# A recommendation tower on one core: two selected pairs of unit 1 go in front, into the banks of the turns, and the last unit's grams get other neighbours

## The chip, the cores and the metric

The kernel runs on one core of one Trainium2 chip. The metric is the device time of one execution in microseconds. Three executions of the kernel before took 426.69, 427.25 and 428.56 us; the median, 427.25 us, is the time before.

## The reference

2048 samples, 32 fields. Every sample takes one row of 64 numbers from each of 32 tables, forms the inner products of all pairs of these 32 rows, and puts them with 16 dense features through a tower of three layers.

```python
e = jnp.stack([tbl_0[ids[:, 0]], ..., tbl_31[ids[:, 31]]], axis=1)   # (2048, 32, 64)
gram = jnp.einsum('bnd,bmd->bnm', e, e)
rows, cols = jnp.triu_indices(32, k=1)
z = gram[:, rows, cols]                                              # 496 products per sample
h = jnp.concatenate([z, dense_ctx], axis=1)                          # 512
h = jnp.maximum(h @ W_top1 + b_top1, 0.0)                            # 512 -> 512
h = jnp.maximum(h @ W_top2 + b_top2, 0.0)                            # 512 -> 256
y = h @ W_top3                                                       # 256 -> 1
```

All numbers are float32. 20 of the tables have 1000 or 1250 rows, 12 are looked up by address.

## The kernel before, in words

The batch is cut into four units of 512 samples (UNITS, UNIT). For each unit the engines do five things.

**Selected fields.** The 20 small tables lie in the on-chip memory, each split into three bf16 parts. VectorE writes one-hot matrices (`one_hots`, a ring of four pieces), and TensorE multiplies them with the tables (`select(u, g)`). Fields go in ten pairs, g = 0 to 9; a pair is worked in two halves. The first seven pairs have 24 matmuls in a half, the last three 30. A pair fills one bank of the accumulator memory. `sel_bank` says which: the two banks of `sel_ps` in turn, but for unit 1's pairs 2 and 3, which go to the two banks of `tower_ps`. ScalarE copies a bank to `vecs` (`selected`, four copies) and counts `sel_emptied`.

**Gathered fields.** GpSimd issues 48 gathers per unit (`gather`, numbered 0 to 191 through the kernel); TensorE transposes the rows in three turns per round (`turn(u, r, x)`, r = 0, 1), into the two banks of `gat_ps`, and ScalarE copies them out (`gathered`, counting `gat_emptied`). After each gather stand some tiny memsets (`spacer`) that hold the next one back. The table `BEHIND` names gathers that wait until a given chunk of grams (unit, round, chunk) is done.

**Grams.** `gram(u, r, c)` is a chunk of 64 small float32 matmuls of 32x32, which the trace shows as 128 matmul records, since each is carried out in two parts. Four chunks make a round, two rounds a unit. Two chunks fill `gram_ps`, which ScalarE, and VectorE for some, copy out.

**The way through HBM.** SyncE's queue writes the products of a unit (`rows_out`, 12 transfers) and reads their diagonals back as `z` (`rows_back`, one transfer of dense features, five of diagonals). The last unit does this round by round, so it has two passes of the tower, of 256 samples each; they are passes 3 and 4, which the code calls LAST and LAST + 1. `rows_back` of either waits until all four blocks of layer 1 of pass 2 are computed, and for the products.

**The tower.** `layer1(v, j)`, j = 0 to 3, `layer2(v, o)`, o = 0, 1, and `layer3(v)`, in the two banks of `tower_ps`, with ScalarE taking each result out.

The order on every engine is written out by hand. TensorE's puts tower work or selects of the next unit between the chunks of grams. In unit 0 every one of the eight chunks has one half of a select of unit 1 ahead of it, so pairs 0 to 3 of unit 1 are done by the end of unit 0's grams (L588 to L600). ScalarE starts to empty them only when the last chunk of unit 0 is done, because the grams still read `vecs` (`act.wait_ge(gram_full, ...)` in its unit loop). `select(1, 4)`, the next work of TensorE, waits for the bank of pair (1, 0) to be emptied (L497, L498). In unit 3, the last, each chunk has half a block of layer 1 of pass 2 ahead of it; layers 2 and 3 of pass 2 follow the last chunk, and then passes 3 and 4.

## Time and profile before

| | us |
|---|---|
| median of three executions | 427.25 |
| the profiled execution | 428.72 |
| its span, first to last instruction | 426.9 |
| TensorE busy | 384.3 (90%) |
| GpSimd busy | 277.2 (65%) |
| VectorE busy | 230.6 (54%) |
| ScalarE busy | 166.6 (39%) |
| mean granted TensorE clock | 0.992 of 2.4 GHz |

All stretches below are in microseconds from the start of the span. An engine's busy time counts instructions that run; the number in square brackets at the end of a row is how long the engine was idle before it, and what ended that. Where the profile finds no releaser it says "issue".

### The profile page before, as it was taken

How to read it: one execution, taken by the hardware profiler on the slowest of the kernel's cores; microseconds unless marked ns; L12 is line 12 of the kernel's file. 1: busy time of each engine (PE TensorE's matmuls, PEld its weight loads, DVE VectorE, ACT ScalarE, POOL GpSimd, SP SyncE). 2: the span in 40 equal slices, each digit the busy share in tenths (PEclk: the TensorE clock that was granted, in tenths of full speed). 3: DMA queues.
4: the chain of work that ended last, by engine and by line, in shares of the span. 5: the costliest groups of instructions: out<-in, count | busy, mean ns of one | idle time of the engine just before them, and what ended most of it. 6: DMA issues, size and time to landing. Idle time of an engine off the chain costs nothing.

```text
span 426.9 us, 15066 instructions
## 1 busy us (share of the span) xinstructions
PE 384.3 (90%) x6516; PEld 216.1 (51%) x6516; DVE 230.6 (54%) x717; ACT 166.6 (39%) x264; POOL 277.2 (65%) x748
## 2 busy tenths in 40 slices
PE   0677868999959999999999999999999999888998
PEld 0343434555535555555545555566445554555576
DVE  2999999863445987006258987007158982001000
ACT  4347576322128425230354425230354425131222
POOL 6888889854548888556578988555588988300000
PEclk9999999999997999999999999999999999999999
DMA  5953941300107781100077721011077111034510
GB/s 178 381 156 100 302 119 38 73 19 15 20 18 140 161 267 44 20 18 17 17 139 154 227 69 47 16 21 18 18 148 170 28 21 23 14 56 97 96 49 0
DMA packets 38236, 37.51 MB, mean 88 GB/s; under 512 B 13781, under 2 KB 26903, under 8 KB 38042
## 3 DMA queue, kind: packets, MB, share of 16 engines
q1 hardware_dynamic: 31594, 29.04, 27.0%
q0 software_dynamic: 6144, 6.30, 7.2%
q10 hardware_dynamic: 432, 1.21, 0.8%
q8 instruction: 51, 0.84, 0.8%
q14 instruction: 15, 0.12, 0.1%
HBM read 28.45 MB, written 8.09 MB: 86 GB/s over the span
## 4 chain that ended last, share of the span: by engine, by line
PE 76%; DVE 14%; issue 4%; ACT 3%; DMA 2%; DVEq 0%
PE sel_ps L511 40%; PE tower_ps L555 13%; DVE onehot L458 10%; PE gram_ps L540 10%; PE tower_ps L565 6%; PE gat_ps L525 3%; PE tower_ps L511 3%; DVE tabs L446 2%; ACT vecs L321 2%; PE tower_ps L574 2%; DVE work L441 2%; DMA ids_wide<-ids_scratch 1%; DMA ids_scratch<-sel_f 1%; DMA sel_ids<-in_ids_sel_dram 1%; ACT tabs L314 0%
## 5 line engine op out<-in xcount | busy, mean ns | idle before, releaser
L458 DVE TENSOR_SCALAR onehot<-ids_wide,row_ids 128x512 bf16<-128x512 f16 x688 | 202.0, 365 | 99.1 <-PE sel_ps L511 80.5
L511 PE MATMUL sel_ps<-onehot,tabs 128*64 128x512 bf16 x1968 | 224.9, 385 | 31.7 <-DVE onehot L458 16.2
L284 POOL DMA_INDIRECT rows<-in_tbl_dram,gat_ids x192 | 195.2, 1017 | 75.7 <-PE gram_ps L540 54.8
L511 PEld LDWEIGHTS sel_ps<-onehot,tabs 128*64 128x64 bf16 x1968 | 117.7, 111 | 133.6 <-issue 36.5
L321 ACT COPY vecs<-sel_ps 64x256 f32<-64x256 f32 x152 | 92.1, 606 | 102.7 <-PE sel_ps L511 58.4
L280 POOL MEMSET spare<- 128x1 f32 x548 | 81.8, 149 | 20.6
L555 PE MATMUL tower_ps<-work,w_sb 128*128 128x512 f32 (+1 forms) x160 | 59.4, 516 | 0.0
L540 PEld LDWEIGHTS gram_ps<-vecs 64*32 64x32 f32 x4096 | 38.9, 105 | 29.8 <-issue 27.0
L540 PE MATMUL gram_ps<-vecs 64*32 64x32 f32 x4096 | 43.9, 201 | 8.1 <-issue 7.1
L555 PEld LDWEIGHTS tower_ps<-work,w_sb 128*128 128x128 f32 x160 | 28.9, 190 | 18.6 <-issue 16.6
L465 DVE COPY work<-gram_ps 128x512 f32<-128x512 f32 x8 | 5.2, 688 | 56.6 <-PE gram_ps L540 56.6
L344 ACT ACTIVATE h<-tower_ps,b_sb 128x512 f32<-128x512 f32 (+1 forms) x20 | 12.0, 602 | 51.6 <-PE tower_ps L555 51.6
L565 PE MATMUL tower_ps<-h,w_sb 128*128 128x512 f32 (+1 forms) x80 | 29.7, 516 | 0.0
L338 ACT COPY work<-gram_ps 128x512 f32<-128x512 f32 x24 | 13.0, 589 | 39.0 <-PE gram_ps L540 39.0
L314 ACT CAST tabs<-work 128x1024 bf16<-128x1024 f32 (+1 forms) x10 | 11.1, 1109 | 25.2 <-DVE work L441 19.5
L329 ACT COPY vecs<-gat_ps 128x512 f32<-128x512 f32 x24 | 13.8, 594 | 14.6 <-PE gat_ps L525 14.3
L565 PEld LDWEIGHTS tower_ps<-h,w_sb 128*128 128x128 f32 x80 | 14.6, 190 | 9.2 <-issue 8.1
L525 PE MATMUL gat_ps<-ident,rows 128*128 128x128 f32 x96 | 14.9, 284 | 0.7 <-ACT vecs L329 0.7
L441 DVE TENSOR_TENSOR work<-work,tabs 128x1024 f32<-128x1024 f32 (+1 forms) x10 | 12.9, 1294 | 2.8 <-ACT tabs L309 2.8
L525 PEld LDWEIGHTS gat_ps<-ident,rows 128*128 128x128 f32 x96 | 10.1, 140 | 7.0 <-issue 5.8
L446 DVE TENSOR_TENSOR tabs<-work,tabs 128x1024 bf16<-128x1024 f32 (+1 forms) x10 | 12.9, 1294 | 1.1 <-ACT tabs L314 1.1
L309 ACT CAST tabs<-work 128x1024 bf16<-128x1024 f32 (+1 forms) x10 | 11.1, 1108 | 5.0 <-DMA work<-in_packed_dram 4.8
(16 smaller groups left out, 41.4 us busy)
## 6 DMA issues: line engine op xcount, KB each, us to landing
ids_wide<-ids_scratch SPq DMA_DIRECT2D x40, 256.0 KB
rows<-in_tbl_dram,gat_ids POOLq DMA_INDIRECT x192
products<-work SPq DMA_DIRECT2D x12, 248.0 KB
products<-work SPq DMA_DIRECT2D x24, 120.0 KB
work<-in_packed_dram SPq DMA_DIRECT2D x5, 512.0 KB
work<-products SPq DMA_DIRECT2D x9, 256.0 KB
work<-in_packed_dram SPq DMA_DIRECT2D x3, 640.0 KB
work<-in_packed_dram ACTq DMA_DIRECT2D x2, 512.0 KB
```

Of the source, the lines that this page charges most:

```text
L280: nc.gpsimd.memset(spare[:], 0.0).then_inc(spaced, 1)
L284: nc.gpsimd.indirect_dma_start(out=rows[:, r, k, h, :], out_offset=None, in_=tables[GATHERED[k]], in_offset=bass.IndirectOffsetOnAxis(ap=g ...
L321: last = nc.scalar.copy(vecs[DIM * h:DIM * h + DIM, :, N_GAT + 2 * g + at], sel_bank(u, g)[DIM * at:DIM * at + DIM, HALF * h:HALF * h + HALF])
L329: nc.scalar.copy(vecs[:, P * r:P * r + P, at:at + fields], gat_ps[:, n % 2, 0:P * fields].rearrange("p (f j) -> p j f", f=fields))\
L441: nc.vector.tensor_tensor(piece, piece, tabs[:, c0:c0 + k, 0, :], ALU.subtract).then_inc(rest_ready, 1)
L446: nc.vector.tensor_tensor(tabs[:, c0:c0 + k, 2, :], stage[g % STAGE_SLOTS][:, 0:k, :], tabs[:, c0:c0 + k, 1, :], ALU.subtract).then_inc(ta ...
L458: last = nc.vector.tensor_scalar(onehot[:, n % RING, c - c0, :], ids_wide[:, k, :], row_ids[chunks[k]][:, c:c + 1], None, ALU.is_equal)
L511: last[at] = nc.tensor.matmul(sel_bank(u, g)[DIM * at:DIM * at + DIM, :], tabs[:, first_chunk[k] + c, part, :], onehot[:, piece_no(u, g, h ...
L525: last = nc.tensor.transpose(gat_ps[:, n % 2, P * at:P * at + P], rows[:, r, k, :, :].rearrange("p h d -> p (h d)"), ident[:])
L540: last = nc.tensor.matmul(gram_ps[32 * s:32 * s + 32, h, i, :], v, v, start=True, stop=True, skip_group_check=True)
L555: last = nc.tensor.matmul(tower_ps[:, (v + j) % 2, 0:width], w1_sb[:, c, P * j:P * j + P], z[:, c, x0:x0 + width], start=(c == 0), stop=(c ...
L565: last = nc.tensor.matmul(tower_ps[:, (v + o) % 2, 0:width], w2_sb[:, j, P * o:P * o + P], h1[:, j, 0:width], start=(j == 0), stop=(j == J ...
```

## The change

Two edits, and the tables that follow from them.

**Unit 1.** `sel_bank` puts pairs 4 and 5 of unit 1 into the banks of `gat_ps`, whose last turn of unit 0 comes before. TensorE's order in round 1 of unit 0 now holds pairs 2 and 3, pair 4 and pair 5 of unit 1: pair 2 whole ahead of chunk 0, then a half ahead of each of chunks 1 to 3, then one and a half pairs behind. The first two turns of unit 1 wait until ScalarE has emptied pairs 4 and 5; pairs 6 and 7 wait for the banks of pairs 0 and 1. VectorE copies the last two chunks of unit 0 out between the halves of pair 5, not of pair 4.

**Last unit.** A whole block of layer 1 of pass 2 stands ahead of each chunk of round 0, and layer 2 and layer 3 of pass 2 are spread ahead of the four chunks of round 1 and of its last. ScalarE's order follows.

**Gathers.** The gates in `BEHIND` move by one or two gathers. Gathers 48 to 63 have one memset behind them (48 to 61 before), 64 to 88 two (three before).

```diff
-NEAR_SPACERS, SPACERS = 1, 3
-NEAR_SPACED = range(48, 62)
+SPACERS = 3
+FEWER = {**dict.fromkeys(range(48, 64), 1), **dict.fromkeys(range(64, 89), 2)}
...
-          56: (0, 1, 0), 58: (0, 1, 1), 60: (0, 1, 2), 62: (0, 1, 3),
+          58: (0, 1, 0), 60: (0, 1, 1), 62: (0, 1, 2), 64: (0, 1, 3),
...
-            return tower_ps[:, g - 2, :] if u == 1 and g in (2, 3) else sel_ps[:, sel_no(u, g) % 2, :]
+            if u == 1 and g in (2, 3):
+                return tower_ps[:, g - 2, :]
+            if u == 1 and g in (4, 5):
+                return gat_ps[:, g - 4, :]
+            return sel_ps[:, sel_no(u, g) % 2, :]
...
+                    layer2(u - 1, (0,))
                 gram(u, 1, 0, (0, 1) if u < LAST else (0,))
                 if u == LAST:
-                    layer1(u - 1, 3)
+                    layer2(u - 1, (1,))
+                    layer3(u - 1)
                     gram(u, 1, 1, (0,))
...
-                    if u == 1 and g == 4:
+                    if u == 1 and g == 5:
                         gram(0, 1, 1, (0, 1))
...
                 if u == 1 and g in (4, 5) and parts[0] == 0:
-                    pe.wait_ge(sel_emptied, n - 3)
+                    pe.wait_ge(gat_emptied, gat_no(0, 1, N_TURNS - 1) + 1)
+                elif u == 1 and g in (6, 7) and parts[0] == 0:
+                    pe.wait_ge(sel_emptied, n - 5)
...
-                if n >= 2:
+                if u == 1 and r == 0 and x < 2:
+                    pe.wait_ge(sel_emptied, sel_no(1, 5 if n % 2 == 1 else 4) + 1)
+                elif n >= 2:
                     pe.wait_ge(gat_emptied, n - 1)
...
                     for c in range(CHUNKS):
-                        layer1(u - 1, c // 2, (c % 2,))
+                        layer1(u - 1, c)
                         gram(u, 0, c)
                     for x in range(N_TURNS):
                         turn(u, 1, x)
-            for c in range(CHUNKS):
-                layer1(LAST - 1, 2 + c // 2, (c % 2,))
-                gram(LAST, 1, c)
+                    layer2(u - 1, 0)
+                    gram(u, 1, 0)
+                    layer2(u - 1, 1, range(0, J1 // 2))
+                    gram(u, 1, 1)
+                    layer2(u - 1, 1, range(J1 // 2, J1))
+                    gram(u, 1, 2)
+                    layer3(u - 1)
+                    gram(u, 1, 3)
```

TensorE, round 1 of unit 0 in the order before: after the last chunk of round 0, one half of a select (24 matmuls) ahead of each of four chunks, and then pairs 4 to 7 in `sel_ps` up to the first turn of unit 1.

```order
L511 MATMUL tower_ps<-onehot,tabs 64x512 x24
L540 MATMUL gram_ps<-vecs 32x32 x64
L511 MATMUL tower_ps<-onehot,tabs 64x512 x24
L540 MATMUL gram_ps<-vecs 32x32 x64
L511 MATMUL tower_ps<-onehot,tabs 64x512 x24
L540 MATMUL gram_ps<-vecs 32x32 x64
L511 MATMUL tower_ps<-onehot,tabs 64x512 x24
L540 MATMUL gram_ps<-vecs 32x32 x64
L511 MATMUL sel_ps<-onehot,tabs 64x512 x204
```

The same place in the order after; `gat_ps` holds pairs 4 and 5.

```order
L513 MATMUL tower_ps<-onehot,tabs 64x512 x48
L544 MATMUL gram_ps<-vecs 32x32 x64
L513 MATMUL tower_ps<-onehot,tabs 64x512 x24
L544 MATMUL gram_ps<-vecs 32x32 x64
L513 MATMUL tower_ps<-onehot,tabs 64x512 x24
L544 MATMUL gram_ps<-vecs 32x32 x64
L513 MATMUL gat_ps<-onehot,tabs 64x512 x24
L544 MATMUL gram_ps<-vecs 32x32 x64
L513 MATMUL gat_ps<-onehot,tabs 64x512 x72
L513 MATMUL sel_ps<-onehot,tabs 64x512 x108
```

One more half stands ahead of the last chunk, and behind it three more halves need no bank that ScalarE has yet to empty.

TensorE, round 1 of the last unit in the order before, from its transposes to layer 1 of pass 3 (L555 is layer 1, L565 layer 2, L574 layer 3).

```order
L525 MATMUL gat_ps<-ident,rows 128x128 x12
L555 MATMUL tower_ps<-work,w_sb 128x512 x2
L540 MATMUL gram_ps<-vecs 32x32 x64
L555 MATMUL tower_ps<-work,w_sb 128x512 x2
L540 MATMUL gram_ps<-vecs 32x32 x64
L555 MATMUL tower_ps<-work,w_sb 128x512 x2
L540 MATMUL gram_ps<-vecs 32x32 x64
L555 MATMUL tower_ps<-work,w_sb 128x512 x2
L540 MATMUL gram_ps<-vecs 32x32 x64
L565 MATMUL tower_ps<-h,w_sb 128x512 x8
L574 MATMUL tower_ps<-h,w_sb 1x512 x2
L555 MATMUL tower_ps<-work,w_sb 128x256 x16
```

The same place after (L559, L569, L578 are the three layers).

```order
L559 MATMUL tower_ps<-work,w_sb 128x512 x4
L544 MATMUL gram_ps<-vecs 32x32 x64
L529 MATMUL gat_ps<-ident,rows 128x128 x12
L569 MATMUL tower_ps<-h,w_sb 128x512 x4
L544 MATMUL gram_ps<-vecs 32x32 x64
L569 MATMUL tower_ps<-h,w_sb 128x512 x2
L544 MATMUL gram_ps<-vecs 32x32 x64
L569 MATMUL tower_ps<-h,w_sb 128x512 x2
L544 MATMUL gram_ps<-vecs 32x32 x64
L578 MATMUL tower_ps<-h,w_sb 1x512 x2
L544 MATMUL gram_ps<-vecs 32x32 x64
L559 MATMUL tower_ps<-work,w_sb 128x256 x16
```

Layers 2 and 3 of pass 2 stood between the last chunk and pass 3, and now stand ahead of it; pass 3 follows the last chunk directly.

## Rows read from the trace of the kernel before

**Rows 1.** The page: busy time by engine, granted clock in 40 slices, instruction queue.
```profile
PE 384.3 (90%) x6516; PEld 216.1 (51%) x6516; DVE 230.6 (54%) x717; ACT 166.6 (39%) x264; POOL 277.2 (65%) x748
...
PEclk9999999999997999999999999999999999999999
...
q8 instruction: 51, 0.84, 0.8%
```

**Rows 2.** TensorE in order of time: start, us, line and what xcount, [idle before <-releaser].
```profile
114.00 0.97 PE L540 MATMUL gram_ps<-vecs 64*32 64x32 f32 x88 [0.37 <-issue]
...
125.27 0.26 PE L540 MATMUL gram_ps<-vecs 64*32 64x32 f32 x6 [1.99 <-issue]
128.07 18.43 PE L511 MATMUL sel_ps<-onehot,tabs 128*64 128x512 bf16 x144 [2.54 <-issue]
147.13 3.21 PE L511 MATMUL sel_ps<-onehot,tabs 128*64 128x512 bf16 x28 [0.64 <-DVE onehot L458]
```

**Rows 3.** ScalarE in order of time, the copies of unit 1's pairs 0 and 1.
```profile
125.58 4.86 ACT L321 COPY vecs<-sel_ps 64x256 f32<-64x256 f32 x8 [9.50 <-PE gram_ps L540]
```

**Rows 4.** By stretch: length, busy (count) of five engines, granted clock, DMA share, GB/s.
```profile
126.00:127.00 1.00, 0.00 (x0) 0.00 (x0) 1.00 (x3) 0.98 (x3) 0.94 (x3) 0.54 0.00 0
...
132.00:133.00 1.00, 1.00 (x8) 0.52 (x6) 0.00 (x0) 0.96 (x3) 0.85 (x2) 0.55 0.88 189
```

**Rows 5.** The chain that ended last, in order of time: start, us, what.
```profile
106.33 2.71 PE tower_ps L511 x24
...
147.13 6.67 PE sel_ps L511 x60
...
168.75 3.44 PE tower_ps L555 x8
172.19 1.22 PE gram_ps L540 x80
```

**Rows 6.** TensorE in order of time, round 1 of the last unit, as rows 2.
```profile
378.27 1.88 PE L555 MATMUL tower_ps<-work,w_sb 128*128 128x512 f32 x4
...
384.28 0.64 PE L540 MATMUL gram_ps<-vecs 64*32 64x32 f32 x51 [0.20 <-issue]
...
388.28 0.68 PE L540 MATMUL gram_ps<-vecs 64*32 64x32 f32 x55 [0.69 <-issue]
...
392.01 0.71 PE L540 MATMUL gram_ps<-vecs 64*32 64x32 f32 x59 [0.42 <-issue]
392.65 7.13 PE L565 MATMUL tower_ps<-h,w_sb 128*128 128x512 f32 x16
```

**Rows 7.** By stretch, as rows 4: round 0 of unit 1, round 0 of the last unit.
```profile
168.75:187.96 19.21, 19.21 (x546) 10.27 (x545) 1.78 (x7) 6.32 (x11) 10.56 (x34) 1.00 0.10 19
...
360.28:375.94 15.66, 12.85 (x531) 7.36 (x529) 0.00 (x0) 5.16 (x9) 6.21 (x20) 1.00 0.07 16
```

**Rows 8.** SyncE's queue in order of time: unit 0's products, then the last unit's.
```profile
126.90 0.32 SPq L191 DMA_DIRECT2D products<-work  x1
...
146.46 0.43 SPq L213 DMA_DIRECT2D work<-products  x1
...
377.26 0.32 SPq L191 DMA_DIRECT2D products<-work  x1
...
405.08 1.25 SPq L209 DMA_DIRECT2D work<-products  x3
```

**Rows 9.** By stretch, as rows 4: the DMA engines while the last transfers land.
```profile
389.00:390.00 1.00, 1.00 (x3) 0.52 (x4) 0.00 (x0) 0.00 (x0) 0.00 (x0) 1.00 0.30 45
390.00:391.00 1.00, 1.00 (x35) 0.24 (x34) 0.00 (x0) 0.09 (x1) 0.00 (x0) 1.00 0.00 0
...
408.00:409.00 1.00, 1.00 (x7) 0.87 (x6) 0.00 (x0) 0.27 (x1) 0.00 (x0) 1.00 0.16 44
```

**Rows 10.** TensorE in order of time, layer 1 of pass 3 and of pass 4.
```profile
401.52 7.17 PE L555 MATMUL tower_ps<-work,w_sb 128*128 128x256 f32 x32
...
413.24 7.17 PE L555 MATMUL tower_ps<-work,w_sb 128*128 128x256 f32 x32
```

More of the change, by code:

```diff
@@ L300, in _ @@
                     gather(u, r, x, k, h)
-                    for _ in range(NEAR_SPACERS if len(of_unit) * u + n in NEAR_SPACED else SPACERS):
+                    for _ in range(FEWER.get(len(of_unit) * u + n, SPACERS)):
                         spacer()
@@ L391, in _ @@
                     layer1(u - 1, 0)
-                    if u < LAST:
-                        layer1(u - 1, 1)
+                    layer1(u - 1, 1)
                 gram(u, 0, 0, (0, 1))
                 if u > 0:
-                    if u < LAST:
-                        layer1(u - 1, 2)
-                        layer1(u - 1, 3)
-                    else:
-                        layer1(u - 1, 1)
+                    layer1(u - 1, 2)
+                    layer1(u - 1, 3)
                 if u == 0:
@@ L408, in _ @@
                 if u == LAST:
-                    layer1(u - 1, 2)
+                    layer2(u - 1, (0,))
                 gram(u, 1, 0, (0, 1) if u < LAST else (0,))
                 if u == LAST:
-                    layer1(u - 1, 3)
+                    layer2(u - 1, (1,))
+                    layer3(u - 1)
                     gram(u, 1, 1, (0,))
@@ L422, in _ @@
                     selected(u + 1, 1)
-            layer2(LAST - 1)
-            layer3(LAST - 1)
             for v in (LAST, LAST + 1):
@@ L581, in _ @@
             for u in range(UNITS):
-                for g in range(4 if u == 1 else 2, N_PAIRS):
+                for g in range(6 if u == 1 else 2, N_PAIRS):
                     select(u, g)
@@ L597, in _ @@
                         gram(0, 0, c)
-                    for c in range(CHUNKS):
-                        select(1, 2 + c // 2, (c % 2,))
-                        gram(0, 1, c)
+                    select(1, 2)
+                    gram(0, 1, 0)
+                    select(1, 3, (0,))
+                    gram(0, 1, 1)
+                    select(1, 3, (1,))
+                    gram(0, 1, 2)
+                    select(1, 4, (0,))
+                    gram(0, 1, 3)
+                    select(1, 4, (1,))
+                    select(1, 5)
                     pe.wait_ge(w_in, 16 * 5)
@@ L625, in _ @@
                         turn(u, 1, x)
-            for c in range(CHUNKS):
-                layer1(LAST - 1, 2 + c // 2, (c % 2,))
-                gram(LAST, 1, c)
-            for v in (LAST - 1, LAST, LAST + 1):
-                if v >= LAST:
-                    for j in range(J1):
-                        layer1(v, j)
+                    layer2(u - 1, 0)
[6 more added lines that the diff above has]
+                    gram(u, 1, 3)
+            for v in (LAST, LAST + 1):
+                for j in range(J1):
+                    layer1(v, j)
                 layer2(v, 0)
```

6 rows, old and new, of the table BEHIND are left out of this document.

## The prediction, made before the changed kernel was run

> **What bounds the kernel now.** I read the page first, then the chain that ended last, then TensorE in order of time at the two places of the change, then SyncE's queue and the DMA share at the end. The page shows TensorE busy for 384 of 427 us and a clock that dips in one slice alone, the thirteenth [rows 1]. So time is to be had only where TensorE stands still or runs at the lower clock, and an edit costs time only where it makes TensorE do so.
>
> There is one large stop. In the last chunk of unit 0's grams TensorE halts for 1.99 us with 6 records to go, ends the chunk at 125.53, and halts again for 2.54 us before pair 4 of unit 1 at 128.07 [rows 2]. The profile names no releaser for either. The second is the bank: ScalarE begins the eight copies of pairs 0 and 1 at 125.58, eight in 4.86 us, so four end at about 128.0 [rows 3], just when TensorE starts. During it the granted clock falls from full (2.4 GHz) to half (1.2 GHz), some 2.8 us after the first halt; it comes back near 132.9 [rows 4]. Between 128.07 and 147.13 TensorE does six halves of 24, which are worth 6 x 2.71 = 16.3 us [rows 5], in 19.1 us: 0.6 us is a wait for one-hots just before pair 7 [rows 2], 2.2 us the clock. From 147.13 to 168.75 it is never late [rows 5].
>
> The first stop, and the smaller ones inside other chunks, I read as instruction supply. PE and PEld together hold 13,032 instructions in 51 packets of the instruction queue [rows 1]: 256 in a packet, or 128 matmul records with their weight loads. From the restart at 114.00 to that at 125.27 stand 88 + 24 + 128 + 24 + 122 = 386 records, three packets: 3.76 us each [rows 2]. From 384.28 to 392.01 stand 51 + 4 + 128 + 4 + 69 = 256 records, two packets: 3.87 us each, the first of them 4.00 [rows 6]. I take 3.8 us as the least time for a packet. A chunk with a half-block ahead is 132 records and would run in 3.1 us (1.9 [rows 6] + 1.2 [rows 5]), so it starves; a chunk with a whole block ahead is 136 records in 4.8 us [rows 7] and does not. Rows 7 show it: four chunks with whole blocks take 19.21 us, all of it busy; with half-blocks 15.66 us, of which 12.85 are busy.
>
> **Unit 1, the front.** Times are on the trace's own scale. Up to 106.26 nothing moves. Then two halves of pair 2 run back to back to 111.8 (5.4 us; the one-hots of the second were written by then, VectorE being two halves ahead). The four chunks and three more halves are 584 records. Without a limit they take 4 x 1.25 (1.22 [rows 5] and a bit at a border) + 3 x 2.71 = 13.1 us and end at 124.9. With the limit: the packet borders fall at the same counts as now, which puts the first 40 records into chunk 0, at 112.2; four packets of 3.8 us follow, to 127.4, and the last 32 records take 0.3: 127.7. I take 127.7; the ends are 124.9 and, with the longest spacing of the rows, 4.00 us, 128.5.
>
> At that point nine halves of unit 1 are done, not eight, and three more need no bank that is full: pair 4's second half and pair 5. These last 3 x 2.71 = 8.1 us, and ScalarE empties pairs 0 and 1 in 4.9 us from the end of the chunk [rows 3], so pair 6 does not wait, and TensorE is never idle long enough for the clock. From 127.7 remain five halves of 24 and the rest: 13.55 us, 0.6 us for the one-hots, and the 21.6 us from 147.13 to 168.75 [rows 5], 35.7 us together. Layer 1 in unit 1 starts at 163.4, not 168.75: **-5.4 us** (-8.2 to -4.5).
>
> What else moves there, at nothing: the first turn of unit 1 comes at about 149 and waits for pair 4 to be copied; ScalarE reaches it after pairs 0 to 4, 5 x 2.43 = 12.2 us after 127.7, at 140. VectorE's copy of the last chunks moves behind one more half and starts at most 3.5 us later than at 125.6, so SyncE's 12 stores start at 130.4, not 126.9 [rows 8], and z lands by about 152, eleven us before layer 1 wants it. That cover gone, it would cost what it is late. GpSimd's gates stay behind a chunk each; the last gathers of unit 1 now leave behind chunk 3 of its round 0, and two turns and a whole pair (2 x 2.71 us [rows 5]) still lie between that and the turn that reads them. I count zero, and no gain: if a gather were late, it would cost 1 to 2 us in one unit.
>
> **The last unit.** Everything there is 5.4 us earlier; I go on in the trace's times and add that at the end. Round 0 takes 19.2 us in place of 15.66 [rows 7], so +3.5 us, for two whole blocks (7.6 us of work) that are moved forward: 4 us of starving and waiting go. The transposes keep their 2.3 us. Round 1 starts at 381.8: layer 2's first output 3.44 us, then 0.6 us to a packet border, at 385.9; three packets follow. Before, the three there took 11.1 us (from about 380.9, worked back from 384.28 by 77 records, half a block and 47 records, to 392.01 [rows 6]); with that they end at 397.0, and 79 records at 0.75 us give 397.8 for the end of the grams, not 392.72: +5.1 us. Without any limit it would be 395.8, at 4.00 us a packet 398.6.
>
> What follows the grams decides. The last chunk ends at 392.72, the stores are issued after it, the loads of z for pass 4 are issued from 405.08 [rows 8] and the DMA engines fall silent early in the slice from 408 [rows 9]; I put the arrival at 408.5, 15.8 us after the grams (15.5 to 16.3). Now layers 2 and 3 of pass 2 (8.87 us) and pass 3 (11.7 us, 401.52 to 413.24 [rows 10]) lie over it, and it is 4.7 us early. After the change only pass 3 does. TensorE is through at 397.8 + 11.7 = 409.5, and z is there at 397.8 + 15.8 = 413.6: a new wait of 4.1 us, whatever the grams' own end. Pass 4 starts at 413.6, not 413.24: **+0.3 us** (-1.7 to +1.1; the stores and loads themselves are unchanged).
>
> Is pass 3's own z there at 397.8? Its stores start at 377.26 + 3.5 = 380.8; the products before were in by 389.7, 12.4 us after the start [rows 8, 9], and loads take 3.4 us: 396.6. Early by 1.2 us, and a small miss is covered by the 4.1 us wait.
>
> The 4.1 us wait is the second place where TensorE stands still. In unit 0 the clock fell some 2.8 us into a halt and half speed cost 2.2 us after it [rows 4]. So I price a fall before pass 4 at **+2.2 us**, and lean to it, since the halt is longer than what it took there, though that one had weak gram work before it, and this one full-width tower work.
>
> The Trainium skill, "TensorE: Matmul & The Clock Gate", section Part 1: The HAM clock gate, says that the throttled clock is the default and that sustained activity releases it; the rows above agree. It would make a fall here likely and no certainty, as the halt may end first.
>
> Sum: -5.4 + 0.3 + 2.2 = -2.9 us. Against the profiled execution, 428.72 us (span 426.9), that is 425.8 us (span 424.0). The median of the runs shown lies 1.5 us lower, at 427.25: **424.3 us**.
>
> **The rivals.**
> *The clock holds before pass 4.* For: the halt of 4.1 us is not much longer than 2.8 us. Then -5.1 us: 422.1 us. 28%.
>
> *Instruction supply isn't the limit.* If the halts inside chunks came from something that the new order removes, the front ends at 124.9 and gives -8.2, the last unit's grams end at 395.8 and give -1.7, and the clock still falls: -7.7 us, 419.6 us. Against it: the even spacing of the restarts over 128 records. 7%. The Trainium skill, "Runtime: NRT & Kernel Launch", section Instruction fetch mechanics, speaks for this one: it calls the crossing of a 16 KiB border mostly hidden. Its block of 256 instructions agrees with the 256 counted here; that it is hidden, rows 7 contradict.
>
> *The clock falls in the front too.* The new order leaves halts of about 1.0 and 1.9 us inside two chunks of unit 0's round 1, among small matmuls. If the clock falls there as it did at 126, its 2.2 us are paid after all: -2.9 + 2.2 = -0.7, 426.5 us. For: one of the halts before the fall was itself of 2 us [rows 2]. Against: round 0 of the last unit is idle for 2.8 of 15.66 us, in pieces, at a full clock [rows 7]. 15%.
>
> *Slower: the drain of the last round, now uncovered.* All of the way through HBM beyond 11.7 us is now TensorE's wait. In unit 0 the same way took from 125.53 to the last load's issue at 146.89 [rows 2, 8] and about 1.2 us to land, 22.6 us. If the last round's took that, pass 4 would start 6.8 us later: -2.9 + 6.8 = +3.9, 431.2 us. It decides from a drain of about 21 us on. Against: this round moves half of unit 0's bytes and took 15.8 us. 7%.
>
> **How the numbers follow.** The forecast has 43%, with its own range 422.3 to 425.9 (front -4.5 to -6.4, end -0.9 to +1.1, the clock 2.2 or somewhat less). 0.5% is 2.1 us, about what a measurement can tell from no change: faster means below 425.1. Faster: four fifths of the forecast (0.34), the held clock (0.28), the third (0.07), 0.01 of the last two: 0.70. Slower: the drain, and 0.02 of the case with two falls: 0.09. The rest, 0.21, is no change. The range of 421.0 to 426.8 leaves out the case without a limit, the drain and the edges of two others, about 0.2.
>
> **What would show it.** Front: no halt of 2.5 us between unit 0's last chunk and pair 4 of unit 1, the clock full throughout, layer 1 in unit 1 near 163.4, halts of 1 to 2 us inside two chunks of unit 0's round 1. Last unit: round 0 near 19.2 us without halts, grams ending about 22 us after its transposes, TensorE idle about 4 us before pass 4, ended by the transfer of z, and the clock at half after it (or not: the first rival). Wrong would be: layer 1 in unit 1 later than 166, a drain other than 15.8 us, or pass 3 waiting for its z by more than 1 us.

## The result: 454.5 us, 6% slower, against 424.3 us predicted

Four runs of the changed kernel took 454.53 us in the median (453.29 to 456.41), the kernel before 427.47 us beside them (426.69 to 428.56): a ratio of 1.0635, 95% interval 1.0591 to 1.0679. The prediction had said 424.3 us, 421.0 to 426.8. Of the 27 us by which it is slower than the kernel before, the profile puts 22 in one place that the prediction had costed at nothing.

The page of the kernel after, busy time by engine and the granted clock, as [rows 1]: the span is 452.8 us (profiled run 454.63 us), TensorE has the same 6516 matmul records, and the clock now dips in slices 13 to 15, 136 to 170 us, and in the last but one.

```profile
PE 392.4 (87%) x6516; PEld 217.6 (48%) x6516; DVE 228.8 (51%) x717; ACT 166.7 (37%) x264; POOL 269.6 (60%) x719
...
PEclk9999999999998659999999999999999999999979
```

TensorE in order of time at the first place of the change, to be held against [rows 2] (columns as there; select is line 513, grams 544, layer 1 559):

```profile
112.64 1.19 PE L544 MATMUL gram_ps<-vecs 64*32 64x32 f32 x108 [0.49 <-issue]
...
123.21 0.26 PE L544 MATMUL gram_ps<-vecs 64*32 64x32 f32 x6 [1.22 <-issue]
...
126.11 1.46 PE L544 MATMUL gram_ps<-vecs 64*32 64x32 f32 x128
127.50 8.08 PE L513 MATMUL gat_ps<-onehot,tabs 128*64 128x512 bf16 x72
136.89 2.32 PE L513 MATMUL sel_ps<-onehot,tabs 128*64 128x512 bf16 x19 [1.31 <-issue]
139.37 0.38 PE L513 MATMUL sel_ps<-onehot,tabs 128*64 128x512 bf16 x1 [0.16 <-issue]
140.10 0.41 PE L513 MATMUL sel_ps<-onehot,tabs 128*64 128x512 bf16 x2 [0.36 <-issue]
...
148.20 3.76 PE L513 MATMUL sel_ps<-onehot,tabs 128*64 128x512 bf16 x14 [6.26 <-issue]
...
165.97 9.59 PE L513 MATMUL sel_ps<-onehot,tabs 128*64 128x512 bf16 x60 [6.65 <-DVE onehot L458]
```

Up to 135.6 this is the forecast: the grams of unit 0 end at 127.5 (127.7 was said), the three halves behind them run in 8.08 us, the halt of 2.54 us at a full bank is gone. Then TensorE all but stops for 30 us. For much of that its records trickle, one or two at a time, 0.72 us apart. The waits by releaser between 127 and 170 us say what it lacked (us in total, times, longest):

```profile
PEld sel_ps L513 <- issue: 28.6, 26, 7.1
DVE onehot L458 <- remote: 23.9, 3, 14.2
ACT vecs L326 <- remote: 22.3, 2, 16.4
```

VectorE waits to write one-hots and ScalarE to copy, both on releases for which the profile finds no engine ("remote"). The chain of the whole run has the same two stretches; layer 1 of unit 1 stands at 190.51 in it, where [rows 5] have 168.75 and the prediction 163.4:

```profile
136.74 9.09 another core or an unknown queue
148.15 14.13 another core or an unknown queue
...
190.51 3.44 PE tower_ps L559 x8
```

One thing runs on all the while, GpSimd's gathers. The changed table of spacers puts two memsets instead of three behind gathers 64 to 88, and they leave 1.36 to 1.46 us apart, every 1.36 us while VectorE stands still (GpSimd in order of time):

```profile
138.19 0.94 POOL L289 DMA_INDIRECT rows<-in_tbl_dram,gat_ids  x1
139.13 0.27 POOL L285 MEMSET spare<- 128x1 f32 x2
139.55 0.94 POOL L289 DMA_INDIRECT rows<-in_tbl_dram,gat_ids  x1
```

The same stretch of the kernel before has three memsets and mostly 1.6 to 1.75 us:

```profile
137.17 1.00 POOL L284 DMA_INDIRECT rows<-in_tbl_dram,gat_ids  x1
138.17 0.46 POOL L280 MEMSET spare<- 128x1 f32 x3
138.78 1.04 POOL L284 DMA_INDIRECT rows<-in_tbl_dram,gat_ids  x1
```

The last gather of that run, 88, leaves at 161.6, and at 162.4 VectorE and soon after everyone moves again. SyncE is not held: its twelve stores of unit 0 are issued in 16.0 us (129.7 to 145.7), in the kernel before in 15.1.

The last unit, answering to [rows 6, 7, 8, 10]: TensorE in order of time from the last chunk on.

```profile
419.25 0.88 PE L544 MATMUL gram_ps<-vecs 64*32 64x32 f32 x79 [0.80 <-issue]
420.06 7.17 PE L559 MATMUL tower_ps<-work,w_sb 128*128 128x256 f32 x32
...
430.62 1.23 PE L578 MATMUL tower_ps<-h,w_sb 128*1 128x256 f32 x4
436.79 9.53 PE L559 MATMUL tower_ps<-work,w_sb 128*128 128x256 f32 x32 [4.94 <-DMA work<-products]
```

Layer 1 starts at 381.49, the grams end at 420.1, 38.6 us later, and pass 4 starts 55.3 us after layer 1, where [rows 7, 10] gave 413.24 - 360.28 = 53.0. The wait for z is 4.9 us and layer 1 behind it takes 9.53 us instead of 7.17. By stretch (as [rows 4]) the granted clock is the lower level, 1.2 GHz, behind that wait:

```profile
432.00:436.00 4.00, 0.00 (x0) 0.00 (x0) 0.00 (x0) 0.25 (x1) 0.00 (x0) 0.84 0.43 128
437.00:440.00 3.00, 3.00 (x8) 2.38 (x9) 0.00 (x0) 0.00 (x0) 0.00 (x0) 0.50 0.00 0
```

From the start of layer 1 to the end of the span are 71.3 us, before 66.6: the last unit costs 4.7 us, and 21.8 us are lost by layer 1 of unit 1. Together that is 26.5 us; what lies between is 0.6 us shorter than before, and the spans differ by 25.9.

### The profile page after: what moved, and what is told of

Its sections match the earlier page's. It is cut to its first block, busy times and chain, and to the rows that moved or that the text cites. A ratio compares the mean times of both kernels' runs of the same rounds, so it can differ in the third digit from the quotient of the medians.

```text
span 452.8 us, 15037 instructions
## 1 busy us (share of the span) xinstructions
PE 392.4 (87%) x6516; PEld 217.6 (48%) x6516; DVE 228.8 (51%) x717; ACT 166.7 (37%) x264; POOL 269.6 (60%) x719
## 4 chain that ended last, share of the span: by engine, by line
PE 69%; DVE 15%; another core or an unknown queue 5%; DMA 4%; ACT 2%; issue 2%; SPq 2%; DVEq 0%
PE sel_ps L513 35%; PE tower_ps L559 12%; DVE onehot L458 11%; PE gram_ps L544 9%; PE tower_ps L569 5%; PE gat_ps L529 3%; PE tower_ps L513 2%; DVE tabs L446 2%; PE gat_ps L513 2%; DVE work L441 2%; ACT vecs L326 2%; PE tower_ps L578 1%; DMA ids_wide<-ids_scratch 1%; DMA products<-work 1%
## 5 line engine op out<-in xcount | busy, mean ns | idle before, releaser
L513 PE MATMUL sel_ps<-onehot,tabs 128*64 128x512 bf16 x1872 | 220.9, 389 | 47.6 <-DVE onehot L458 22.7
L513 PEld LDWEIGHTS sel_ps<-onehot,tabs 128*64 128x64 bf16 x1872 | 111.8, 112 | 151.7 <-issue 59.5
L326 ACT COPY vecs<-sel_ps 64x256 f32<-64x256 f32 x144 | 87.3, 606 | 114.7 <-PE sel_ps L513 54.3
L285 POOL MEMSET spare<- 128x1 f32 x519 | 74.2, 143 | 18.9
L559 PE MATMUL tower_ps<-work,w_sb 128*128 128x512 f32 (+1 forms) x160 | 60.8, 532 | 4.9 <-DMA work<-products 4.9
L544 PEld LDWEIGHTS gram_ps<-vecs 64*32 64x32 f32 x4096 | 38.9, 105 | 26.7 <-issue 26.5
L559 PEld LDWEIGHTS tower_ps<-work,w_sb 128*128 128x128 f32 x160 | 30.9, 201 | 25.3 <-issue 17.2
L569 PE MATMUL tower_ps<-h,w_sb 128*128 128x512 f32 (+1 forms) x80 | 30.1, 517 | 0.0
L569 PEld LDWEIGHTS tower_ps<-h,w_sb 128*128 128x128 f32 x80 | 14.5, 190 | 8.3 <-issue 7.2
```

What stands on the lines that cost most here:

```text
L285: nc.gpsimd.memset(spare[:], 0.0).then_inc(spaced, 1)
L326: last = nc.scalar.copy(vecs[DIM * h:DIM * h + DIM, :, N_GAT + 2 * g + at], sel_bank(u, g)[DIM * at:DIM * at + DIM, HALF * h:HALF * h + HALF])
L513: last[at] = nc.tensor.matmul(sel_bank(u, g)[DIM * at:DIM * at + DIM, :], tabs[:, first_chunk[k] + c, part, :], onehot[:, piece_no(u, g, h ...
L544: last = nc.tensor.matmul(gram_ps[32 * s:32 * s + 32, h, i, :], v, v, start=True, stop=True, skip_group_check=True)
L559: last = nc.tensor.matmul(tower_ps[:, (v + j) % 2, 0:width], w1_sb[:, c, P * j:P * j + P], z[:, c, x0:x0 + width], start=(c == 0), stop=(c ...
L569: last = nc.tensor.matmul(tower_ps[:, (v + o) % 2, 0:width], w2_sb[:, j, P * o:P * o + P], h1[:, j, 0:width], start=(j == 0), stop=(j == J ...
```

## The experiments

Twelve kernels ran. Two theories stood at the start: the closer gathers hold back what the other engines tell each other, or the pairs moved in front, in the banks of the turns, stall something. Each time is a median, with its ratio to the kernel before measured beside it.

**e1, the change with three memsets.**

```diff
-FEWER = {**dict.fromkeys(range(48, 64), 1), **dict.fromkeys(range(64, 89), 2)}
+FEWER = dict.fromkeys(range(48, 64), 1)
```

> The changed kernel with one number put back: three memsets again behind the gathers 64 to 88 (two in the changed kernel, three before). Nothing else differs. In the changed kernel TensorE, VectorE and ScalarE stand still for most of 136 to 166 us of the trace, while SyncE's product stores and unit 1's gathers run; it starts layer 1 of unit 1 at 190.5 us. Theory P (the closer gathers, together with the stores, are what holds the other engines up): the stall goes, layer 1 of unit 1 starts near 163.5, and the time is that of before, 427.5, less 5.4 in front plus 4.6 lost at the end = about 427 us (424 to 430). Theory Q (the new order itself, or the place of the stores against it, causes the stall, whatever the gathers' pace): 450 to 456 us, layer 1 of unit 1 near 190.

432.35 us (428.67 to 435.0), ratio 1.0092 [1.0056, 1.0128]. 22 us come back with 25 memsets, and the long stall is gone. Layer 1 of unit 1 starts at 163.2, as predicted; TensorE in order of time:

```profile
163.18 3.60 PE L559 MATMUL tower_ps<-work,w_sb 128*128 128x512 f32 x8
```

The time itself is a miss, 2.4 us above the 424 to 430 us that theory P gave: with 5.4 us won there and 4.6 lost at the end the kernel should have been as fast as before. e3, e4, e8 and e9 take that up.

**e2, the kernel before with two memsets.**

```diff
-  for _ in range(NEAR_SPACERS if n in NEAR_SPACED else SPACERS):
+  for _ in range(NEAR_SPACERS if n in NEAR_SPACED else 2 if 62 <= n < 90 else SPACERS):
```

(n stands for the gather's number over all units, here and below.)

> The kernel before with one number changed: two memsets in place of three behind the gathers 62 to 89. Order and banks are those of before. Theory P (pace of the gathers beside the stores): a stall of 10 to 22 us in unit 1, 437 to 450 us. Theory Q (the order): no such stall, 426 to 429 us. If both are needed, 427 as well, with the first experiment at 427 too.

451.36 us (445.59 to 451.6), 1.0488 [1.0399, 1.0577], 1 us over the 437 to 450 that theory P gave. The stall is there without any pair moved, so the theory of the moved pairs falls. Its waits between 127 and 172 us:

```profile
DVE onehot L458 <- remote: 21.6, 3, 11.8
ACT vecs L321 <- remote: 19.1, 1, 19.1
```

**e5 and e6, e2 in two halves:** two memsets behind gathers 62 to 74 (over unit 0's stores), and behind 75 to 89 (over the loads and after them).

```diff
...
+  2 if 62 <= n < 75 else SPACERS     (e5)
+  2 if 75 <= n < 90 else SPACERS     (e6)
```

> The kernel before with two memsets in place of three behind the gathers 62 to 74 only: these are issued at about 126 to 147 us of the trace, while SyncE's 12 product stores of unit 0 (short rows, many packets) are on their way. Gathers 75 to 89 keep three. Theory S (closer gathers beside the stores make the stall): most of it is here, 436 to 452 us. Theory L (it is the loads of z and of ids_wide behind the stores, 146 us on): 427 to 429. Theory G (gathers at 1.4 us apart in any company): both this and the next stall.

> The kernel before with two memsets in place of three behind the gathers 75 to 89 only, issued at about 147 to 170 us, beside the loads of z and of ids_wide (up to 158 us) and then alone. Theory S: no stall, 426 to 429 us. Theory L or G: 434 to 450 us.

e5 437.86 us, 1.0248 [1.019, 1.0305]; e6 439.87 us, 1.0295 [1.0228, 1.0361]: 10 and 12 us, together 22 of e2's 23, from two executions each. It isn't one collision with one transfer, which is what theory G said; theories S and L both fall. In e5 the gathers go on with three memsets from 143.5 us, and VectorE works again for good from 149.9. In e6 TensorE is still starved when the DMA engines are nearly idle, in the second of these stretches; by stretch (TensorE's busy time first, the DMA share before the last number):

```profile
158.00:163.00 5.00, 3.11 (x27) 1.33 (x27) 1.94 (x7) 2.12 (x4) 4.49 (x11) 1.00 0.47 110
163.00:168.00 5.00, 2.28 (x14) 0.99 (x14) 2.86 (x10) 0.00 (x0) 4.39 (x12) 0.93 0.12 27
```

**e10, the spacing kept by one long memset** in the kernel before: one of 512 columns instead of three of 1, a gather every 1.81 us.

```diff
-  spare = sb("spare", [P, 1], F32)
+  spare = sb("spare", [P, 512], F32)
...
+  for _ in range(1 if 48 <= n < 90 else SPACERS):
+      spacer(512 if 62 <= n < 90 else 1)
```

> The kernel before with one memset of 512 columns in place of the three of one column behind the gathers 62 to 89; by the 128-column memset of the trace (0.20 us, 0.10 for one column) it lasts about 0.5 us, so gathers stand some 1.55 to 1.7 us apart, as with three. Theory R (the spacing in time counts): 426 to 430 us. Theory N (it is the number of small instructions with their semaphores between gathers that counts): a stall as with two memsets or longer, 440 us and more.

438.2 us, 1.0235 [1.0203, 1.0267], from two executions: a miss of both theories (426 to 430, and 440 and more), and slow for another reason. No wait on a "remote" release is left between 127 and 172 us. So few memsets between gathers do not make the stall. What costs is VectorE, which takes 45% of the chain between 120 and 200 us, in the kernel before 4%: its one-hots (by line, 136 to 157 us) take 524 ns each,

```profile
L459 DVE TENSOR_SCALAR onehot<-ids_wide,row_ids 128x512 bf16<-128x512 f16 x47 | 21.1, 524 | 0.0
```

where the kernel before has them, 136 to 167 us, at 370 ns (they overlap: by the busy time one ends every 0.45 us in e10 and every 0.30 before):

```profile
L458 DVE TENSOR_SCALAR onehot<-ids_wide,row_ids 128x512 bf16<-128x512 f16 x91 | 27.1, 370 | 4.4 <-PE sel_ps L511 3.1 <-issue 1.2
```

The Trainium skill, "GPSIMD Engine Reference", section Architecture, says that GpSimd's physical read and write port of SBUF is shared with VectorE. These rows agree with that, 524 ns beside 370, though no run here shows that the port is what costs.

**e3, the new last unit alone,** with its gates, all else as before.

```diff
-                    if u < LAST:
-                        layer1(u - 1, 2)
-                        layer1(u - 1, 3)
-                    else:
-                        layer1(u - 1, 1)
+                    layer1(u - 1, 2)
+                    layer1(u - 1, 3)
...
-            for c in range(CHUNKS):
-                layer1(LAST - 1, 2 + c // 2, (c % 2,))
-                gram(LAST, 1, c)
+                    layer2(u - 1, 0)
+                    gram(u, 1, 0)
+                    layer2(u - 1, 1, range(0, J1 // 2))
+                    gram(u, 1, 1)
```

> The kernel before with only the last unit's new order (whole blocks of layer 1 ahead of round 0's chunks, layers 2 and 3 ahead of round 1's) and its gates. By the trace of the changed kernel, counted from layer 1's start in the last unit to pass 4's start: 55.1 us, 53.0 before, and half speed after the wait costs 2.4 more. So both theories on the front expect +4.6 us: 432.1 us (430.5 to 433.5). If this part were worth what the prediction gave it, +2.5: 430.0.

432.36 us (429.23 to 433.87, 10 runs), 1.0097 [1.0071, 1.0123]: 4.4 us slower, as expected. Its profile is of the quickest of the ten runs, so the median run has some 3 us more than these lines (TensorE in order of time):

```profile
396.41 7.17 PE L550 MATMUL tower_ps<-work,w_sb 128*128 128x256 f32 x32
...
412.05 8.86 PE L550 MATMUL tower_ps<-work,w_sb 128*128 128x256 f32 x32 [3.85 <-DMA work<-products]
```

The grams end 38.6 us after layer 1 started (357.92), z comes 15.6 us after them, 11.7 us of pass 3 cover it, and the clock is half behind the wait. In this profile pass 4 starts 54.1 us after layer 1, 1.2 us later than in the kernel before, and layer 1 behind the wait takes 1.7 us more: 2.9 us. The same two terms are 2.3 and 2.4 us in the profile of the change.

**e4, the new front alone,** with its gates, three memsets, and the last unit of before.

```diff
-FEWER = {**dict.fromkeys(range(48, 64), 1), **dict.fromkeys(range(64, 89), 2)}
+FEWER = dict.fromkeys(range(48, 64), 1)
...
+(the last unit's order and its gates 189, 190, 191 as in the kernel before)
```

> The changed kernel's front (pairs 4 and 5 ahead, in the banks of the turns, its gates) with three memsets behind the gathers from 64 on, and the last unit's order of before. Theory P: no stall, layer 1 of unit 1 near 163.5: 422 us (420.5 to 424), faster than both kernels. Theory Q: about 449 us.

428.5 us (427.26 to 431.82), 1.002 [0.9987, 1.0053], 6.5 us over what I expected. The gain is there and is given back. TensorE in order of time:

```profile
163.99 3.60 PE L564 MATMUL tower_ps<-work,w_sb 128*128 128x512 f32 x8
167.52 0.59 PE L549 MATMUL gram_ps<-vecs 64*32 64x32 f32 x45
168.36 0.28 PE L549 MATMUL gram_ps<-vecs 64*32 64x32 f32 x5 [0.25 <-issue]
169.10 0.35 PE L549 MATMUL gram_ps<-vecs 64*32 64x32 f32 x15 [0.46 <-issue]
169.90 0.27 PE L549 MATMUL gram_ps<-vecs 64*32 64x32 f32 x6 [0.45 <-issue]
170.64 0.86 PE L549 MATMUL gram_ps<-vecs 64*32 64x32 f32 x57 [0.47 <-issue]
171.43 4.88 PE L564 MATMUL tower_ps<-work,w_sb 128*128 128x512 f32 x8
```

The first chunk of unit 1 takes 4.0 us instead of 1.3, and the block behind it 4.88 instead of 3.70, the granted clock being 0.61 and 0.54 in the two stretches from 170 to 174. Beside that chunk GpSimd issues gathers 87 and 88 (167.79 and 169.31). In the kernel before the gathers were through by then, the last issued at 170.87 and the chunk begun at 172.12: TensorE came 5 us later, GpSimd did not come earlier. e1 has the same chunk, with the same two gathers, in 3.98 us.

**e8 and e9, the spacing of those last gathers changed** in e4: two memsets behind 81 to 88, four behind 84 to 88.

```diff
-FEWER = dict.fromkeys(range(48, 64), 1)
+FEWER = {**dict.fromkeys(range(48, 64), 1), **dict.fromkeys(range(81, 89), 2)}     (e8)
+FEWER = {**dict.fromkeys(range(48, 64), 1), **dict.fromkeys(range(84, 89), 4)}     (e9)
```

> The changed kernel's front with the last unit's order of before (the fourth experiment), and two memsets in place of three behind the gathers 81 to 88 only, which go out at 157 to 169 us, when stores and loads are through. The fourth experiment won 5.4 us up to layer 1 of unit 1 and lost 4 of them in the first chunk after it, because gathers 86 to 88 still went out beside that chunk. Here the last of them is issued 2.1 us earlier, at about 167.2. Theory C (gathers beside an instruction-hungry chunk hold TensorE up): the halts in that chunk halve, the clock holds, 425.5 to 427 us. Theory G (closer gathers anywhere stall all engines): 430 us and more.

> The fourth experiment (the changed front, three memsets, the last unit of before) with four memsets behind the gathers 84 to 88, those that stand beside the end of unit 1's selects and its first chunk of grams, where VectorE is idle and three memsets let a gather out every 1.52 us, not every 1.65 to 1.7. Theory R (what holds the other engines is the rate: a gather needs some 1.6 us of something shared, and only a closer spacing starves them): the halts of 0.46 us in that chunk go though one or two gathers more now stand beside it, the clock holds, and the front keeps most of its 5.4 us: 423 to 425 us. Theory C (any gather beside such a chunk costs it): as the fourth experiment or worse, 428 to 430 us.

e8: 427.21 us, 0.9991 [0.9959, 1.0023], just over what theory C gave. The chunk has no halts, and no gather is issued beside it. But a small stall of the long one's kind stands ahead of it, with waits on "remote" releases of 7.0 us on ScalarE and 3.3 on VectorE, so eight closer gathers are enough for one: theory G is right in kind, and wrong in its 430 us; TensorE in order of time:

```profile
168.97 1.34 PE L549 MATMUL gram_ps<-vecs 64*32 64x32 f32 x128 [2.08 <-ACT vecs L326]
170.24 5.20 PE L564 MATMUL tower_ps<-work,w_sb 128*128 128x512 f32 x8
```

e9: 428.51 us, 0.9998 [0.9973, 1.0022]. The gathers beside the chunk are now 1.67 us apart, not 1.52, and it still has four halts of 0.45 to 0.47 us and the half clock behind. So for a chunk it is not this step in spacing that counts: **any gather beside a chunk of small matmuls costs it**, which is theory C.

**e11, e4 with the gates moved** about three gathers earlier in every unit, so that none stands beside chunk (1,0,0). One thing more differs from e4: gathers 92 to 95 have one memset behind them, not three. They go out after chunk (1,0,0), so what is read at that chunk is the gates' doing; no run tells the two edits apart behind it.

```diff
-FEWER = dict.fromkeys(range(48, 64), 1)
+FEWER = {**dict.fromkeys(range(48, 64), 1), **dict.fromkeys(range(92, 96), 1)}
...
-          89: (1, 0, 0), 91: (1, 0, 1), 93: (1, 0, 2), 95: (1, 0, 3),
+          86: (1, 0, 0), 88: (1, 0, 1), 90: (1, 0, 2), 92: (1, 0, 3),
...
-          189: (3, 0, 0), 190: (3, 0, 1), 191: (3, 0, 2)}
+          185: (3, 0, 0), 188: (3, 0, 1), 190: (3, 0, 2)}
```

> The changed front with three memsets between gathers 64 to 88 and the last unit of the kernel before (as e4_front_three, 428.5 us), and every gate of GpSimd's gathers moved about three gathers earlier, so that gathers 86 to 88 no longer stand beside the first gram chunk (1,0,0) of unit 1 but in front of layer 1's end. Theory C (the gathers beside a chunk of small matmuls give back what the front won: the chunk's halts of 0.46 us and the half clock behind it, some 4 us): no halts in chunk (1,0,0), the clock at 0.9 or more between 165 and 175 us, layer 1 of unit 2 at 259.5 to 261 instead of 263.3, and 423 to 424.5 us, 3 to 4 us under the kernel before. Rival G (the gathers and not the chunk are what counts: moved, they are late or in the way in another place, beside chunk (2,0,0) or ahead of turn (1,1,2)): the layer-1 time of unit 2 stays near 263 or comes later, and 426 to 429 us.

425.7 us (424.89 to 426.59, 6 runs), 0.9949 [0.993, 0.9967]: faster than the kernel before and than e4, though 1.2 us short of what theory C expected. Halts and half clock are gone there, and layer 1 of unit 2 comes at 259.30, which is 5.1 us ahead of the kernel before (264.44 by the same view). TensorE in order of time:

```profile
166.53 1.29 PE L549 MATMUL gram_ps<-vecs 64*32 64x32 f32 x128
167.75 3.70 PE L564 MATMUL tower_ps<-work,w_sb 128*128 128x512 f32 x8
...
259.30 3.60 PE L564 MATMUL tower_ps<-work,w_sb 128*128 128x512 f32 x8
```

2 of the 5.1 us were lost again in the last unit, where seven gathers now stood in round 0, two of them beside its second chunk: three halts, and the half-block behind at 3.19 us instead of 1.98.

**e12 and e13, the last unit's gathers.** e12 is e11 with that unit's gates as before (189, 190, 191). e13 lets two more gathers through in unit 2's round 1 and gates 187, 189 and 190 in the last unit.

```diff
-          185: (3, 0, 0), 188: (3, 0, 1), 190: (3, 0, 2)}
+          189: (3, 0, 0), 190: (3, 0, 1), 191: (3, 0, 2)}     (e12)
+          187: (3, 0, 0), 189: (3, 0, 1), 190: (3, 0, 2)}     (e13, with 147, 149, 151, 153 for unit 2)
```

> e11_gates (425.7 us; layer 1 of unit 2 at 259.3, 5.3 us ahead of the kernel before, but the pass after the grams only 3.1 us ahead) with the gates of the last unit as in the kernel before (gathers 189, 190 and 191 behind the chunks of round 0). In e11 seven gathers stood in the last unit's round 0, its second chunk had three halts of 0.46 to 0.50 us and the block behind it ran at half clock. Theory C (gathers beside a chunk of the last unit cost its time): now the gathers up to 188 run on without a gate, to about 363, past chunk (3,0,0) and up to the second; the second chunk (3,0,1) is left alone, but the first has two gathers beside it. Halts in chunk 1 gone, round 0 16 to 17 us instead of 18.0, 424 to 425.5 us. Rival (the halts belong to the order of the chunks and half-blocks and not to the gathers): round 0 stays at 18 us and 425.7 us.

> e11_gates with two more gathers let through in round 1 of unit 2 (gates at 147, 149, 151 and 153 instead of 147, 148, 150, 151) and the last unit's gates at 187, 189 and 190, so that five gathers stand in its round 0 instead of seven, none beside a chunk. Theory C: the second chunk of the last unit has no halts of 0.46 us, round 0 takes 15.7 to 16.5 us, 423.2 to 424.5 us. Rival (two gathers to a half-block of round 1 in unit 2 already reach into the chunks there): halts of 0.46 us and half clock in unit 2's round 1, what the last unit wins is lost there, 425 to 427 us.

e12: 431.0 us, 1.007 [1.0043, 1.0098], a miss of both expectations. The first chunk of the last unit is the plainest picture of C: gathers 185 to 188 now run through it. TensorE in order of time:

```profile
359.94 0.58 PE L549 MATMUL gram_ps<-vecs 64*32 64x32 f32 x45 [0.88 <-ACT vecs L326]
360.67 0.27 PE L549 MATMUL gram_ps<-vecs 64*32 64x32 f32 x6 [0.16 <-issue]
361.40 0.39 PE L549 MATMUL gram_ps<-vecs 64*32 64x32 f32 x18 [0.46 <-issue]
362.24 0.27 PE L549 MATMUL gram_ps<-vecs 64*32 64x32 f32 x6 [0.45 <-issue]
...
366.41 3.78 PE L564 MATMUL tower_ps<-work,w_sb 128*128 128x512 f32 x4
```

128 records take 6.5 us instead of 1.28, and the half-block behind them 3.78 instead of 1.98. The records come in bunches every 0.72 to 0.84 us, two bunches for each gather (1.52 us apart); in the long stall the single records were 0.72 us apart too. Round 0 of the last unit takes 21.2 us here, 3.2 more than in e11.

e13: 425.62 us (422.67 to 426.42, 10 runs), 0.9935 [0.991, 0.996]: faster than the kernel before by 0.4 to 0.9%, with e11 the best here, but no better than e11 and over the 423.2 to 424.5 us that C expected. Round 0 of the last unit takes 15.4 us instead of e11's 18.0, as C said. The sign that C named is not there, though: one gather still goes out beside the second chunk (363.18) and one beside the fourth (370.61), each with one halt of 0.46 to 0.48 us, at a full clock. And its profile is 2.3 us behind e11's when that round starts, with a halt of 0.48 us in unit 2's round 1, the rival's mark.

1.5 us of that lag is there at unit 2 already, ahead of the gates that differ, and the profiles show where it comes from. In e12 and e13 the clock fell behind the halt in the third chunk of unit 0's round 1. First e11, then e13, TensorE in order of time:

```profile
123.48 2.78 PE L518 MATMUL gat_ps<-onehot,tabs 128*64 128x512 bf16 x24
123.96 0.26 PE L549 MATMUL gram_ps<-vecs 64*32 64x32 f32 x6 [1.99 <-issue]
124.15 4.47 PE L518 MATMUL gat_ps<-onehot,tabs 128*64 128x512 bf16 x24
```

The granted clock is 0.62 in those 4.47 us, and layer 1 of unit 1 starts 2.3 us later than in e11 (2.9 in e12). The halt is 1.45 us long in e11, where the clock holds, and 1.99 in e13; but in e9 it is 1.99 as well and the clock holds. All four kernels are the same up to there, so this is a difference between executions, and that part of the lag of e12 and e13 does not come from their gates.

## Why the prediction was wrong, step by step

**The step that failed** is the one on GpSimd: "GpSimd's gates stay behind a chunk each (...) I count zero, and no gain: if a gather were late, it would cost 1 to 2 us in one unit." The prediction thought of gathers only as late. It priced the gates and passed over the edit beside them, two memsets for three behind gathers 64 to 88. It had no row on closer gathers, gave no bound from either side, and had no rival for it. That edit is worth 22 us: the change without it takes 432.35 us (e1), and the kernel before with it alone 451.36 us (e2).

**The front** was right in mechanism and size: grams' end at 127.5 (said 127.7), no bank wait, layer 1 of unit 1 at 163.2 in e1 (said 163.4), two halts in the chunks at a full clock (0.49 and 1.22 us, said about 1.0 and 1.9). But -5.4 us as a gain of the kernel was wrong without more edits: e4's profile keeps 1.3 us of it at unit 2, and its median none. What the sum left out is again GpSimd. 25 gathers 1.5 to 1.7 us apart fill the stretch from the gates of unit 0 to unit 1's round 0, so a TensorE that is 5 us ahead meets the last of them in its first chunk, and halts and half clock give 4 us back. With the gates moved (e11) 5.1 us are there at unit 2.

**The last unit** was right in kind and too small: +2.5 us said (0.3 and 2.2), +4.4 us measured (e3). Round 0 took 19.2 us, as said. The terms that were off: the grams ended 38.6 us after layer 1's start (said 37.5), the three halts there being 0.87, 0.69 and 0.80 us; z came 15.6 us (e3) and 16.7 us (the change) behind them, said 15.8. So pass 4 started 54.1 us (e3) and 55.3 us (the change) after layer 1, not 53.3. The clock fell behind the wait as forecast, +2.4 us in the profile after and +1.7 in e3. z of pass 3 was in time. That the wait for z is uncovered once layers 2 and 3 stand ahead of it held in both. So did the halts inside the chunks that the prediction read as instruction supply. Those of the last unit's round 1 cannot be the gathers, since GpSimd is idle there; that they are instruction packets rests on their spacing of 128 records, and no run changed the packets.

**The rivals.** The clock did not hold before pass 4 in the profiles with the new last unit (the change, e1, e3). The halts in the chunks stayed. The clock did not fall in unit 0's chunks in the profiles of the change, e1, e4, e8, e9 and e11, but it did in those of e12 and e13, which have the same front: this rival, given 15%, is a matter of the execution. The drain was not 22.6 us. None of the four had the mechanism that decided, and the slower side, with 9%, rested on the drain and on the clock falling twice.

The sum by the runs: closer gathers 22 us (after against e1), last unit 4.4 (e3), front 0.5 (e4, within its noise of zero), together 26.9; the change measured 27.1.

**What stays open** is why closer gathers do this. The runs show that it follows the spacing in time (1.36 to 1.5 us in a run of gathers stalls, 1.5 to 1.75 with three memsets and 1.65 to 1.81 with one long one don't), that it needs a run of them (the pairs of gathers with one memset in unit 0 are 1.25 to 1.4 us apart and stall nothing; eight were enough in e8), that it goes on when the loads are done (e6), that it reaches three engines at once, and that it ends 1 to 8 us after the last closer gather (the change, e5, e6). Whether the semaphore updates or the instruction packets are what is late was not told apart; for the halts within a chunk, where the wide matmuls ahead go on at full rate, late instructions are the likelier reading, and it is argued, not shown.

## What to carry to other kernels

An engine that issues transfers and is nowhere on the chain can still hold all others: price its pacing as an edit of its own, and bound it by a run in which only the pacing changes. When an early stretch gets shorter, look which other engine filled it exactly; its last work then lands beside the next stage. Here that was worth as much as the whole gain, and moving the gates with the work (e11, e13) turned no change into 0.5 to 0.65% faster. Before stores and loads that are covered by a tower pass are shifted, the cover has to be counted from the last gram and not from the start of the unit.

## What the runs showed of the hardware

- Gathers from GpSimd mostly 1.36 to 1.5 us apart cost 10 us when there are 13 of them (e5), 12 when there are 15 (e6), 22 to 23 when there are 25 to 28 (the change, e2); those 1.5 to 1.75 us apart cost nothing that shows beside wide matmuls. The step between is as small as one memset of one column.
- Beside chunks of small matmuls (10 ns a record) gathers 1.52 or 1.67 us apart bring halts of 0.46 us, mostly two for each gather, and a chunk of 1.28 us took 4.0 (two gathers) to 6.5 us (four).
- In e1, e4, e9, e11 and e12 the clock went to half behind three to eight such halts in one chunk, in pieces of 0.5 us or less each; behind one halt of 0.46 to 0.48 us in a chunk (e13) it did not, nor in the last unit of the kernel before, where halts of 0.2 to 0.8 us are 4 us apart. In e8 it fell behind one wait of 2.1 us ahead of the chunk.
- The halt in the third chunk of unit 0's round 1 was 1.2 to 2.0 us long with the new front, and the clock fell behind it in two profiles of eight.
- A memset of 512 columns on GpSimd slows VectorE's one-hots beside it from 370 to 524 ns.
